# Context attention: all four score matmuls of a sequence behind one wait for the four exponentials before it

## The reference, cut to what matters

```python
def _L1_xattn_ref(x, context, w_qkv, w_proj, b_proj):   # x: 128 x 32 x 128, context: 128 x 257 x 256
    H, D = 16, 8                                        # 16 heads of 8 columns
    q, k, v = (x @ w_qkv.T) in 3 x heads
    extra_k, extra_v = context in 2 x heads
    k = concatenate([extra_k, k]); v = concatenate([extra_v, v])   # 257 + 32 = 289 keys
    attn = softmax((q * D ** -0.5) @ k.T)               # 128 x 16 x 32 x 289
    return (attn @ v) @ w_proj.T + b_proj
```

## Time and profile before

| | us |
|---|---|
| median of three runs | 3559.14 |
| profiled execution, its own time | 3559.38 |
| its span | 3557.5 |
| first to last score matmul of the changed stage, from the span's start | 1025.5 to 1461.1 |

### The profile page before, as it was taken

How to read it: one execution, slowest core, us unless ns; L and a number is a source line. 1 busy time by engine, 2 the same in 40 slices (tenths; PEclk the granted TensorE clock), 3 DMA queues, 4 the chain that set the end, 5 groups by cost and what they waited for, 6 DMA issues and landing times. The chain is left out here.

```text
span 3557.5 us, 110134 instructions
## 1 busy us (share of the span) xinstructions
PE 3208.9 (90%) x41582; PEld 2687.3 (76%) x41584; DVE 2507.1 (70%) x7190; ACT 1835.4 (52%) x4594; POOL 1260.3 (35%) x1887
## 2 busy tenths in 40 slices
PE   6886999999989999888899999999999999873866
PEld 4665999999957777546789889888998899743345
DVE  6784999999968888567455555555555555477765
ACT  4341777787768888574433333333333333343463
POOL 3673888888834343204200000000000000174042
PEclk8996999999989999998799999999999999997677
DMA  4001000000022222100465555555555555374000
GB/s 121 8 2 40 1 0 0 0 0 0 1 70 82 82 83 81 46 1 7 99 145 130 126 127 139 127 130 132 132 131 127 127 136 130 74 134 62 0 3 27
DMA packets 375654, 254.59 MB, mean 72 GB/s; under 512 B 118724, under 2 KB 371608, under 8 KB 374680
## 3 DMA queue, kind: packets, MB, share of 16 engines
q1 hardware_dynamic: 370968, 245.64, 28.4%
q10 hardware_dynamic: 4352, 4.20, 0.5%
HBM read 233.73 MB, written 15.75 MB: 70 GB/s over the span
## 5 line engine op out<-in xcount | busy, mean ns | idle before, releaser
L2482 PE MATMUL psum<-L_xattn_ctxT,L_xattn_q_ctx 128*128 128x257 f32 x2048 | 508.8, 389 | 2.9 <-issue 2.3
L1076 PE MATMUL psum<-L_ffn_share,L_ffn_prob 128*128 128x128 f32 x4096 | 487.9, 278 | 23.1 <-DVE L_ffn_prob L1009 15.6
L893 POOL TENSOR_TENSOR L_ffn_sums<-L_ffn_sims 128x1024 f32<-128x1024 f32 x256 | 485.4, 1913 | 61.2 <-DVE L_ffn_prob L1009 61.2
L2513 PEld LDWEIGHTS psum<-L_xattn_probT,L_xattn_ctx 32*128 32x128 f32 x16384 | 468.9, 187 | 44.5 <-issue 42.0
L1076 PEld LDWEIGHTS psum<-L_ffn_share,L_ffn_prob 128*128 128x128 f32 x4096 | 471.3, 193 | 35.8 <-DVE L_ffn_prob L1009 25.6
L2513 PE MATMUL psum<-L_xattn_probT,L_xattn_ctx 32*128 32x128 f32 x16384 | 493.2, 273 | 2.1 <-DVE L_xattn_probT L2396 2.1
L2334 ACT ACTIVATE L_xattn_prob<-psum,L_xattn_nmax 128x258 f32<-128x258 f32 x512 | 239.2, 472 | 479.9 <-DVE L_xattn_nmax L2382 463.0
L2305 POOL TENSOR_TENSOR L_xattn_z_var<-L_xattn_z_mv,L_xattn_z_eps 128x1 f32<-128x1 f32 x32 | 6.1, 192 | 1245.0 <-DVE L_xattn_z_mv L2408 1215.7
L2482 PEld LDWEIGHTS psum<-L_xattn_ctxT,L_xattn_q_ctx 128*128 128x128 f32 x2048 | 367.3, 190 | 64.8 <-issue 8.2
L935 ACT ACTIVATE psum<-L_ffn_sums,L_ffn_bias 128x512 f32<-128x512 f32 x512 | 339.1, 686 | 64.8 <-DVE L_ffn_prob L1009 60.3
L1009 DVE SCALAR_TENSOR_TENSOR L_ffn_prob<-L_ffn_sums,L_ffn_best,psum 128x512 f32<-128x512 f32 x512 | 358.1, 741 | 7.0 <-ACT psum L935 3.4
(11 more groups left out here) (463 smaller groups left out, 6504.0 us busy)
## 6 DMA issues: line engine op xcount, KB each, us to landing
L_xattn_ctx<-ctx_dram SPq DMA_DIRECT2D x512, 256.0 KB, 3.8
L_xattn_ctxT<-ctx_T_dram SPq DMA_DIRECT2D x128, 257.0 KB, 3.3
L_xattn_k_all<-ctx_T_dram SPq DMA_DIRECT2D x128, 128.5 KB, 2.1
L_xattn_v_all<-ctx_dram SPq DMA_DIRECT2D x128, 128.0 KB, 2.2
L_attn_qkv_scratch<-L_attn_qkv SPq DMA_DIRECT2D x24, 256.0 KB, 3.2
L_attn_rows<-L_attn_qkv_scratch SPq DMA_DIRECT2D x24, 256.0 KB, 5.3
start_raw<-ctx_dram ACTq DMA_DIRECT2D x16, 256.0 KB, 11.9
L_xattn_v_rows<-L_xattn_v SPq DMA_DIRECT2D x8, 256.0 KB, 2.3
```

What stands on the lines that cost most here:

```text
L893: nc.gpsimd.tensor_tensor(sums[:, h % RING, :, :], sx, sy, ALU.add).then_inc(summed, 1)
L1076: last = nc.tensor.matmul(pair(2 * s)[:, c * P:(c + 1) * P], prob[:, h % RING, c * P:(c + 1) * P], share[:, h % RING, :], start=(h == 0 an ...
L2482: last = nc.tensor.matmul(scores(s)[:, g, 0:CTX], q_ctx[:, p, c, b, h:h + 4, :].rearrange("p h n -> p (h n)"), ctxT[:, b, c, :], start=(c ...
L2513: last = nc.tensor.matmul(mix_bank(r)[:, c * P:(c + 1) * P], ctx[rows, b, k, c * P:(c + 1) * P], probT[rows, b % 2, k, :, :].rearrange("p ...
```

## The change

The two pairs become one loop. All four score matmuls of n wait for `exped` of n-1; none starts on the second exponential any more. DVE's first maximum waits for `scored`, that is, for all four groups. The semaphores `scored_low` and `exped_low` and the waits on them are gone. Nothing else changes: the same matmuls, maxima and exponentials on the same data, in the same order on each engine.

```diff
 # ACT, exps
                     ins = nc.scalar.activation(prob[:, b % 2, g, :], scores(g), ACT.Exp, bias=nmax[:, b % 2, g:g + 1],
                                                accum_out=total[:, b % 2, g:g + 1])
-                    if g == 1:
-                        ins.then_inc(exped_low, 1)
                 ins.then_inc(exped, 1)
 # DVE, maxes
-                dve.wait_ge(scored_low, t * BT + b + 1)
+                dve.wait_ge(scored, t * BT + b + 1 + BT)
                 for g in range(G):
-                    if g == 2:
-                        dve.wait_ge(scored, t * BT + b + 1 + BT)
                     nc.vector.tensor_reduce(nmax[:, b % 2, g:g + 1], scores(g), X, ALU.max, negate=True).then_inc(maxed, 1)
 # PE
-            def score_pair(t, b, pair):
-                for g in (2 * pair, 2 * pair + 1):
-                    rows = slice(32 * g, 32 * g + 32)
-                    ins = nc.tensor.matmul(scores(g), q_bd[rows, b % 2, :, :].rearrange("p j w -> p (j w)"),
-                                           k_all[rows, b, :], start=True, stop=True)
-                return ins
-
             def score(t, b, before):
                 pe.wait_ge(k_in[b], (t + 1) * 16)
                 pe.wait_ge(prepared, t * BT + b + 1)
                 if before:
-                    pe.wait_ge(exped_low, t * BT + b)
-                score_pair(t, b, 0).then_inc(scored_low, 1)
-                if before:
                     pe.wait_ge(exped, t * BT + b)
-                score_pair(t, b, 1).then_inc(scored, 1)
+                for g in range(G):
+                    rows = slice(32 * g, 32 * g + 32)
+                    ins = nc.tensor.matmul(scores(g), q_bd[rows, b % 2, :, :].rearrange("p j w -> p (j w)"),
+                                           k_all[rows, b, :], start=True, stop=True)
+                ins.then_inc(scored, 1)
```

More of the change, by code:

```diff
@@ L1263, in context_attention @@
         ends_in = [core.sem(f"{name}_ends_in{pair}") for pair in range(BT // 2)]
-        (zeroed, prepared, scored_low, scored, maxed, exped_low, exped, ended, inverted, spread_out, turned0, turned1, turned_tail, copied0, copied1,
+        (zeroed, prepared, scored, maxed, exped, ended, inverted, spread_out, turned0, turned1, turned_tail, copied0, copied1,
          end_copied, mixed, joined, out_done) = (core.sem(f"{name}_{n}") for n in (
-             "zeroed", "prepared", "scored_low", "scored", "maxed", "exped_low", "exped", "ended", "inverted", "spread_out", "turned0", "turned1", "turned_tail",
+             "zeroed", "prepared", "scored", "maxed", "exped", "ended", "inverted", "spread_out", "turned0", "turned1", "turned_tail",
              "copied0", "copied1", "end_copied", "mixed", "joined", "out_done"))
```

## The result

The changed kernel took 3577.32 us (median of six, 3570.51 to 3581.81) against 3558.21 us for the kernel before, whose runs were made with it. The ratio is 1.0053, 95% interval 1.0043 to 1.0064: slower, by 19 us. The profiled execution took 3578.11 us, 18.7 over the one of before. A second set of runs of both kernels, on one chip, gave 3576.51 against 3559.37, ratio 1.0055 (1.0041 to 1.0070).

A forecast was written before the change was run, and what follows sets the result against it. PE and DVE were taken as nearly bound (3.03 and 3.05 us a step), waiting in turn with ACT; the closed ring adds 12.1 to 13.0, the start 0.4: +12.9 on 3559.38 gives 3572.3 us, range 3563 to 3579.

The forecast's parts named there:

- The ring: Score, maximum, four exponentials, back to score: 0.80 + 0.50 + 2.04 + 0.06, so no step under 3.40 us after the change.
- The projection step: Once a tile PE sets the length: 3.86 us in place of 4.19, 0.33 less, as the mid-score stall goes.
- the wait itself: From the end of ACT's fourth sum to the first matmul that waits for it: 0.06 us of the 3.40.
- removed waits: One signal fewer on ACT and PE, one wait fewer on PE and DVE: 0 to -1.3 us, taken as 0.
- DVE's wait for the fourth quadrant: DVE's first maximum waits for the fourth quadrant, not the second: up to 0.01 us a step, 3.40 to 3.41.
- The start of the stage: At granted clock 0.50 the second score starts 0.88 us later; half taken, +0.4 us, bounds 0 and +0.9.
- What would show it: Scores of 0.77 to 0.79, steps 3.40 thrice and 3.86, DVE idle 41 us, PE about 35, stage 12 to 13 longer.
- three signs of being wrong: Non-projection step under 3.3, projection step not falling to 3.86, or later stages moving by more than the stage does.
- Four at once pays: Rival: PE's stream alone sets the step and every stall vanishes, -22.8 us, 3536.6 us; chance 0.04.
- The short ring: Rival: ring shorter or mostly there before; at ring 3.29, +2.6 us, 3562.0 us, no measurable change; chance 0.10.
- The clock: Rival: PE standing still drops its clock to 0.50 for a tenth of the sequences, +13.7 on top, 3586 us; chance 0.05.
- The tail of 26.3 ns an increment: Cost per increment after concurrent matmuls, from the skill page: one fewer on the ring's 94 steps would give -2.5 us.

The follow-up runs named there:

- e2: Changed kernel, but the low pair keeps its own signal and DVE starts on it; both pairs still wait for the fourth exponential: 3581.42 us, ratio 1.0062 to before.
- e3: Kernel before, PE still in pairs, but DVE waits for all four groups ahead of its first maximum: 3575.08 us, ratio 1.0044 to before.
- e8: e2 with PE's waits for keys and prepared queries moved away from the score: 3572.11 us, ratio 1.0035 to the kernel before.
- e4: Changed kernel with each exponential over 145 of the 289 columns, a test only: 3549.90 us, ratio 0.9972 to the kernel before.
- e5: Kernel before with each exponential over 145 of the 289 columns, a test only: 3546.16 us, ratio 0.9965 to the kernel before.
- e1: Changed kernel with PE's waits for keys and prepared queries moved ahead of turn_lower, leaving only the exponentials' wait at the score: 3575.68 us, ratio 1.0055 to before.
- e10: e1 again, run beside the changed kernel on one chip: 3575.83 us, ratio 1.0051 to the kernel before.
- e6: Kernel before with the bias added to x by POOL once a tile in place of PE's bias matmul: 3536.65 us, ratio 0.9945 to before.

## Why the prediction was right, and where it was short

*The sign and the mechanism held.* The measured time lies in the range, but 1.7 us from its upper edge: a term of 6 us was missing, and room left for the spread between runs covered it. That the range held is in part luck. The forecast was +12.9 us by a ring through score, maximum and four exponentials that the change closes. The ring is there in the trace (PE, DVE and ACT each wait for the one before), it comes with either half of the change alone (e2, e3), it has the predicted length when nothing is added to it (3.39 in e8, 14.06 a tile in e3), and the loss goes when it is made shorter (e4 against e5).

*The projection step* fell from 4.19 to 3.86, as forecast, in every kernel that packs the score and keeps the bias on PE.

*The term that was too small is the wait itself.* The prediction took 0.06 from the end of the exponentials to the first matmul, from the one row where it could be seen, the high pair's. There the wait stood alone on the weight load. In the changed kernel it shares the place with two others, and in two steps of four it takes 0.15: + 0.10 x 2 x 31 = 6.2 us. The prediction spoke of removed waits (0 to -1.3 us), with "a loss has no reason, since no operation is added". That was the step that failed. None was added, but the wait for the fourth exponential, which had been on the load, became an instruction of its own; with the other waits moved away (e1, e10) the steps fall from 3.52 to 3.42.

*A smaller one:* DVE's wait for the fourth quadrant was put at up to 0.01 and cost 0.03 a step (3.39 in e8, 3.42 in e1). The fourth matmul's last record starts only 0.014 after the second's (1212.220 - 1212.206, single records); the rest is not explained. The step of 3.41 came out anyway where the wait was on the load, because the other terms had been rounded up by 0.01 to 0.02 in all, so about 1 us is left of it over 94 steps. Together 12.9 + 6.2 + 1 make 20, against a stage that grew by 19 to 22 and a median that grew by 19.1. The start of the stage cost 0.6 and 0.4 in the two traces over its first two steps, where 0.4 was forecast.

*What would show it.* The scores last 0.77 and DVE's idle time rose to 51.4 us, where 41 were forecast. PE's idle time released by the exponentials was forecast at 35 us less 0.17 for each score; the waits view has 35.6 and 16.7. "Steps should be 3.40, 3.40, 3.40" was wrong for two of three, and the stage grew by 19 to 22 us, not by 12 to 13. None of the three signs of being wrong came: no step is under 3.3, the projection step fell to 3.86, and what follows the stage moved by 2.

*The rivals.* *Four at once pays* needed the exponentials to end 2.97 after the score began; they end 3.37 after it (1208.29 - 1204.92). The short ring didn't come about. The clock stayed at 0.99 in the stage. The tail of 26.3 ns an increment (the Trainium skill, TensorE: Matmul & The Clock Gate, The cost: per-tile semaphore tail) would have made the changed kernel's ring shorter, as it signals once and not twice. The runs show the reverse: with two signals DVE begins 0.79 to 0.80 after the first matmul (e2), with one 0.83 to 0.84. These differ in which matmul carries the awaited signal too, so they do not measure the tail itself; for this change the measurement decides.

## What to carry to other kernels

Before two waits are merged into the later one, add up the ring that this closes: from the signal, through every engine, back to the signal. Two half-buffers with a signal each let one sequence start under the other; here that was worth 0.6 us a tile of four, though it costs PE 0.3 whenever the second half stalls; packing all four took a score from 1.1 to 0.77 us, which gained 0.33 once a tile and no more. And see where the wait that comes last stands: with the other waits moved to where they are long fulfilled, it sat on the weight load here and cost 0.05 us, not 0.15. That shortened the stage by 5.6 us, and the whole time by nothing that could be told from the spread.

## What the runs showed that was not expected

A wait that stood as an instruction of its own ahead of a weight load with another wait cost 0.10 us more than one on the load (0.15 against 0.05 from the end of ACT's last sum to the score; 3.52 against 3.42 a step, e1).

The matmul of one row of ones against the bias, recorded from 1211.99 to 1212.47, cost PE's stream 0.60 us, more than its own records last, and 31 of them were worth 18 to 19 us of the stage and 21 us in whole time (e6). Taking it away made the next matmul begin 0.22 after the projection (1198.08 - 1197.86), where it had been 0.73 (1212.40 - 1211.67 of the kernel before), and the one after that came 0.24 behind (1198.32 - 1198.08) in place of 0.34 (1212.74 - 1212.40). The Trainium skill (TensorEngine Tiling (Array Packing), Key Properties) says that changing the tiling mode drains the engine. That would fit a one-row matmul between full ones, but no run here separates the drain from the matmul.

The turn of the tile loop cost DVE 0.21 us where nothing hid it (e4, e5), which was seen only once DVE was the bound.
